# One more wait as GpSimd's last instruction: all additions to the result have landed

## The reference

```python
x = x + xattn(layernorm(x), ctx, Wq, bq, Wk, bk, Wv, bv)
x = x + ffn(layernorm(x), Wr, W1, b1, W2, b2)
```

```python
probs = softmax(x @ Wr.T)
top_v, top_i = top_k(probs, 2)
top_v = top_v / sum(top_v)
for e in range(8):
    w_e = sum(where(top_i == e, top_v, 0))
    h = gelu(x @ W1[e].T + b1[e])        # 1024 wide
    out = out + (h @ W2[e].T + b2[e]) * w_e
```

## Time and profile before

| what | us |
|---|---|
| time, median of 3 runs | 350.07 |
| lowest and highest of the 3 | 349.89 to 351.91 |
| time of the profiled execution | 351.43 |
| its span, from the first to the last instruction | 349.7 |
| PE busy in the span | 330.7 (95%) |
| DVE busy | 257.0 (74%) |
| ACT busy | 188.9 (54%) |
| POOL busy | 123.9 (35%) |

### The profile page before, as it was taken

The page is one execution under the profiler, slowest core; times in us unless marked ns, Lnnn a source line. Parts: engine busy times, 40 slices in busy tenths (PEclk is TensorE's granted clock), DMA queues, the critical chain, the costliest instruction groups (busy, mean ns, idle before and its releaser), DMA issues.

```text
span 349.7 us, 8731 instructions
## 1 busy us (share of the span) xinstructions
PE 330.7 (95%) x2648; PEld 268.9 (77%) x2648; DVE 257.0 (74%) x720; ACT 188.9 (54%) x333; POOL 123.9 (35%) x124
## 2 busy tenths in 40 slices
PE   8999999989979979899999999999999999999980
PEld 4556766847646858688888888888899898988870
DVE  4266899879877989898987876567667575767660
ACT  2589969878977982444433344343434353535220
POOL 6008211481382580346534223331322324131332
PEclk9999999999998989999999999999999999999996
DMA  7996975494685327234365433432425243345212
GB/s 236 371 339 186 305 257 180 150 301 139 202 290 171 62 100 220 33 78 105 51 92 64 60 47 39 56 47 47 56 40 76 34 60 47 47 58 53 32 17 30
DMA packets 51112, 41.82 MB, mean 120 GB/s; under 512 B 28541, under 2 KB 46526, under 8 KB 50942
## 3 DMA queue, kind: packets, MB, share of 16 engines
q1 hardware_dynamic: 40798, 27.36, 28.7%
q0 software_dynamic: 7872, 11.77, 18.9%
q10 hardware_dynamic: 2400, 2.13, 1.9%
HBM read 22.28 MB, written 13.86 MB: 103 GB/s over the span
## 4 chain that ended last, share of the span: by engine, by line
PE 71%; DVE 17%; POOL 5%; issue 3%; ACT 1%; POOLq 1%; DVEq 0%
PE o_ps L799 30%; PE s_ps L781 14%; PE t_ps L781 13%; PE s_ps L649 4%; DVE w2l L1268 3%; POOL rows L515 3%; PE proj L683 2%; PE proj L636 2%; DVE w1l L1268 2%; PE o_ps L575 2%; POOL rstd L502 1%; DVE xn L1154 1%; PE proj L611 1%; PE t_ps L659 1%; DVE negmax L1205 1%
## 5 line engine op out<-in xcount | busy, mean ns | idle before, releaser
L547 POOL DMA_INDIRECT out<-y,xm x39 | 61.4, 1575 | 119.3 <-DVE y L1713 111.2
L799 PE MATMUL o_ps<-w2h,gh 128*128 x312 | 85.5, 274 | 1.9 <-DVE gl L1679 1.8
L1055 ACT ACTIVATE g<-s_ps,b_sb,down 128x256 f32<-128x256 f32 (+1 forms) x100 | 45.2, 520 | 75.6 <-PE s_ps L781 75.6
L799 PE MATMUL o_ps<-w2h,gl 128*128 x312 | 85.6, 274 | 0.0
L799 PE MATMUL o_ps<-w2l,gh 128*128 x312 | 85.6, 274 | 0.0
L1055 ACT ACTIVATE g<-t_ps,b_sb,down 128x256 f32<-128x256 f32 (+1 forms) x92 | 42.5, 526 | 41.4 <-PE t_ps L781 40.3
L1677 DVE TENSOR_SCALAR gh<-g,up 128x512 f16<-128x512 f32 x78 | 38.7, 496 | 32.9 <-ACT g L1055 31.7
L1679 DVE SCALAR_TENSOR_TENSOR gl<-g,up,gh 128x512 f16<-128x512 f32 x78 | 58.6, 751 | 2.8
L781 PE MATMUL s_ps<-xT,w1h 128*128 128x256 f16 (+1 forms) x400 | 51.1, 252 | 0.7 <-issue 0.7
L781 PE MATMUL t_ps<-xT,w1h 128*128 128x256 f16 (+1 forms) x368 | 48.3, 255 | 0.6 <-issue 0.6
L515 POOL DMA_INDIRECT rows<-send,place x32 | 37.9, 1184 | 27.0 <-DVE place L1379 14.8
(11 more groups left out here) (226 smaller groups left out, 482.5 us busy)
## 6 DMA issues: line engine op xcount, KB each, us to landing
staged<-W2T SPq DMA_DIRECT2D x8, 1024.0 KB, 7.4
staged<-W1T SPq DMA_DIRECT2D x7, 1024.0 KB, 6.2
rows<-send POOLq DMA_DIRECT2D x8, 260.0 KB, 5.1
x_own<-x SPq DMA_DIRECT2D x2, 512.0 KB, 4.7
w2l<-W1T SPq DMA_DIRECT2D x1, 1024.0 KB, 10.2
out<-x_own ACTq DMA_DIRECT2D x2, 512.0 KB, 5.7
b_sb<-b SPq DMA_DIRECT2D x1, 1024.0 KB, 5.1
out<-y,xm POOLq DMA_INDIRECT x39, 3.8
```

Of the source, the lines that this page charges most:

```text
L547: pool.indirect_dma_start(out=out, out_offset=bass.IndirectOffsetOnAxis(ap=xm[:, t % MB, r, META - 1:META].bitcast(I32), axis=0), in_=y2[: ...
L799: i = nc.tensor.matmul(y_ps[n % 2][:, 0:D], l[:, t % 2, m, r * P:(r + 1) * P], w[:, bass.ds(e, 1), m * D:(m + 1) * D].rearrange("p a n -> ...
L1055: i = nc.scalar.activation(g[:, m, 0:width(t)], h_ps[group % 4][:, at:at + width(t)], ACT.Gelu, bias=b1_sb[:, bass.ds(e, 1), m:m + 1].rear ...
```

## The change

One instruction is added at the end of GpSimd's program, behind the loop that issues the last indirect DMAs. It waits until the semaphore `added` has reached 16 for each of the 39 additions. It is the same condition as SP's at L457. Nothing is removed or moved.

```diff
             pool.wait_ge(stored, 16 * B)
             for t in range(FIRST_LATE, NTILES):
                 scatter(t)
+            pool.wait_ge(added, 16 * BEFORE[NTILES])
 
         @block.tensor
         def _(pe):
```

## The result

The changed kernel takes 353.66 us (median of 8 runs, 352.67 to 358.51), the kernel before 350.26 (8 runs, 349.77 to 356.85). The ratio is 1.0077, with a 95% interval of 1.0041 to 1.0113: slower by 0.4 to 1.1%. One execution of each kernel ran at a lower granted clock and took 5 to 7 us longer (358.51 and 356.85); the medians include it, the ratio and its interval leave it out.

What follows compares the result with a forecast made beforehand. PE was taken to bound nearly all of the span, and POOL's DRAIN its end. DRAIN from 345.65 plus 4.0 us ends at 349.65, +0.2 us; 350.07 + 0.2 = 350.3 us, range 346.0 to 352.9.

Steps and rivals of the forecast that it cites:

- What sets the end: At the block's closing: POOL's DRAIN, 8.852 us to 349.45, alone sets the end of the 349.7 us span.
- The wait's place: Behind POOL's last DMA: the wait binds until 345.5, so POOL's DRAIN starts at 345.65 and not at 340.6.
- The one unknown: How long POOL's closing DRAIN lasts if begun at 345.65 with all DMAs landed; bounded between 0.05 and 6.27 us.
- I take the middle: POOL's closing DRAIN still needs 4.0 us after the last landing, ending at 349.65: +0.2 us; chance 0.40.
- The first rival: POOL's closing DRAIN works through all 80 issued DMAs anew, 78 ns each, 6.27 us: +2.5 us, 352.5; chance 0.25.
- An unseen end of the last DMA instruction: After POOL's last DMA record: part of the 6.27 us could be that instruction still completing, beside the wait; no time change.
- The second rival: POOL's closing DRAIN asks slowly only while transfers are in flight; with all landed, nothing to do: -3.7 us, 346.3; chance 0.25.
- passes of equal length: POOL's closing DRAIN makes whole passes of 3.13 us; after the landing one suffices: -0.7 us, 349.4; chance 0.10.
- The lower bound of 0.05 us: Shortest length allowed for POOL's closing DRAIN begun at 345.65, as for other engines: end at 345.7, -3.7 us.
- The range: Forecast interval for the changed kernel's time, meant to hold 8 times in 10: 346.0 to 352.9 us.

## Why the prediction was wrong

*What sets the end.* Right: it is POOL's DRAIN, and the other engines meet it. PE's part is the same to 0.5 us.

*The wait's place.* Right: I put the start 0.2 us behind the landing; the profile has 346.6 for a landing at 342.65 + 3.8 = 346.45.

*The one unknown.* Wrong. The step that failed is "I take the middle", with its ground that the landing is "the only event between the engine's last instruction and the end of DRAIN", so that a rest of 4.0 us follows it. The 4.0 us were not a part that begins with the landing. They were what was left of a walk of 6.28 us that had begun at 343.18 when the transfer landed 2.25 us later. The nearest row in time was taken for the cause. Begun behind the landing, the DRAIN took 6.277 us and not 4.0, and the wait cost 2.4 us and not 0.2. The landing does bind DRAIN, but only where the walk is shorter than 2.25 us or so, as the kernels with an earlier DRAIN show (end about 0.25 us behind SP's release).

*The first rival* is what happened. Its numbers: 78 ns for each DMA, measured 82 and a few DMAs fewer; DRAIN 6.27, measured 6.277; +2.5 us, measured 2.4 in the profile; 352.5 us against 353.66 and 352.74 measured. What I held against it was that POOL's indirect DMAs take a steady 1.55 us and show no growing bookkeeping. That was no evidence: the bookkeeping is done by DRAIN, not at the issue. What stood for it, a short first DRAIN with no DMA behind it, was the better row: it ties the length to what POOL had issued, and that was the cause.

*An unseen end of the last DMA instruction*, which the prediction allowed for within the 6.27 us, is not in them: the changed kernel's DRAIN began 2.4 us behind that instruction's record (346.6 against 344.20) and still took 6.277 us.

*The second rival*, a slow way of asking while something is in flight, is refuted by the changed kernel itself: nothing is in flight and DRAIN takes 6.277 us. So are *passes of equal length* (3.1 us expected). The lower bound of 0.05 us was a good one (47 ns), but for a DRAIN with no DMA since the last one. The Trainium skill's rule of about 12 ns for the DRAINs at a program's start and end, on all five engines ("VectorE: DVE Perf Modes", "The DRAIN you can't avoid"), holds here for SP (13 ns), and for POOL not even when its DRAIN has nothing to do (47 ns).

*The range* held the first rival's 352.5 and ended 0.4 us above it. The median of the first measurement lay another 0.8 us higher. Of its 3.4 us above the kernel before, the DRAIN accounts for 2.4; for the rest no cause is shown. Single executions of the kernel before lie 2 us apart (349.89 to 351.91 in the three runs shown), and the end of the range should have had that spread added.

## What to carry to other kernels

Where GpSimd has issued DMAs, look at the DRAIN with which its program ends. Here it took about 80 ns for each DMA since the last DRAIN (less where some were large), and this time began when POOL had finished its last instruction and come to the DRAIN. Don't put anything ahead of it that waits (SP can wait for the landings, as it did here); and if the walk is longer than the last landing, issue a DRAIN in an earlier idle stretch of GpSimd, which brought 0.7% here with one line. When a stretch has two possible beginnings (here an engine's end and a landing), the distance from the nearer one isn't evidence for it.

## What the runs showed of the hardware

- POOL's DRAIN: 47 ns with no DMA since the last one, 539 ns with 6, 2417 with 29, 6277 with 80; its length repeated to the nanosecond between executions (6277 in both profiles of the changed kernel, 8852 in two kernels that start it beside the last two DMAs). The first three numbers are on one line of 82 ns for each DMA; 80 DMAs lie 0.3 us below it.
- It also awaits the transfers: in the kernel with one DRAIN earlier and no wait it ended about 0.25 us behind SP's release by the last landing, where the walk alone would have ended near 342.9.
- Large DMAs lengthen it less than small ones do, at the same number of packets (16 large: 0.285 us, 32 large: 1.265 us, 16 small: 1.306 us); why is open.
